# The weights' setup made part of the attention's program, with its maxima over partitions by PE and VectorE

## What is computed

```python
def attn(x, Wv, Wo, Wg, Wb):            # x is normalized
    rk = heads(x); rk = rk / max(norm(rk), 1e-12)
    wk = rk one position later, zeros first
    v = heads(x @ Wv.T); gate = sigmoid(x @ Wg.T); beta = sigmoid(x @ Wb.T)
    for t in time:                      # S is 32 x 32 for each head
        err = (v[t] - wk[t] @ S) * beta[t]
        S = S + outer(wk[t], err)
        o[t] = (rk[t] @ S) * gate[t]
    return o @ Wo.T

def ffn(x, weight, gamma_w, beta_w):
    xn = layernorm(x, eps=1e-3) * gamma_w + beta_w
    beta = mean(abs(weight)); w_q = clip(round(weight / (beta + 1e-5)), -1, 1)
    g = max(abs(xn))                    # over the whole tensor
    return clip(xn * 128 / g, -128 + 1e-5, 128 - 1e-5) @ w_q * (g * beta / 128)
```

## Time and profile before

| | us |
|---|---|
| median of 3 runs | 2226.49 |
| lowest, highest | 2221.43, 2229.44 |
| the profiled execution | 2225.45 |
| its span (first to last instruction) | 2223.7 |
| mean granted TensorE clock of it | 0.972 |

### The profile page before, as it was taken

One profiled execution on the slowest core, in us unless ns is written; L12 is line 12 of the kernel. 1 busy time (PEld: TensorE's weight loads), 2 busy tenths in 40 slices (PEclk: granted clock), 3 DMA queues, 4 the chain that ended last, 5 costly groups with the idle time before them and its releaser, 6 DMA issues. The chain is left out here.

```text
span 2223.7 us, 124254 instructions
## 1 busy us (share of the span) xinstructions
PE 2071.3 (93%) x50216; PEld 1310.2 (59%) x50216; DVE 1976.8 (89%) x5810; ACT 1759.7 (79%) x3756; POOL 1726.0 (78%) x3099
## 2 busy tenths in 40 slices
PE   1689999999999999999999999999999987599997
PEld 1356666666666666666666666666666654355554
DVE  5388999999999999999999999999999993688886
ACT  3668888888888888888888888888888744477775
POOL 2678989989999999999898999998999854244443
PEclk7789999999999999999999999999999998799999
DMA  3123333333333333333333333333333322588885
GB/s 95 45 69 79 99 100 101 100 99 101 100 100 100 100 102 103 103 101 100 99 100 100 100 102 99 101 100 101 99 102 96 88 80 73 180 228 228 228 228 126
DMA packets 171997, 247.78 MB, mean 111 GB/s; under 512 B 54904, under 2 KB 54912, under 8 KB 171424
## 3 DMA queue, kind: packets, MB, share of 16 engines
q1 hardware_dynamic: 171424, 239.85, 40.3%
HBM read 104.40 MB, written 67.11 MB: 77 GB/s over the span
## 5 line engine op out<-in xcount | busy, mean ns | idle before, releaser
L805 DVE TENSOR_TENSOR ps_elim<-ps_elim,sys 128x30 f32<-128x30 f32 (+14 forms) x1920 | 547.7, 331 | 0.7
L813 DVE TENSOR_TENSOR sys<-sys,ps_elim 128x30 f32<-128x30 f32 (+14 forms) x1920 | 539.9, 321 | 1.0
L937 PE MATMUL ps_v<-wv,xt 128*128 128x512 f16 x1536 | 431.5, 391 | 20.5 <-DMA kbd<-kt 14.4
L937 PE MATMUL ps_y<-wo,ot 128*128 128x512 f16 x1536 | 401.4, 384 | 11.0 <-DVE x L866 10.4
L974 PEld LDWEIGHTS ps_chain<-rhs,t_t 32*32 32x32 f32 x16384 | 255.1, 144 | 110.1 <-issue 103.6
L974 PE MATMUL ps_chain<-rhs,t_t 32*32 32x32 f32 x16384 | 282.9, 218 | 5.8 <-DVE rhs L834 4.8
L711 ACT ACTIVATE state<-ps_s 128x512 f32<-128x512 f32 x128 | 76.5, 598 | 239.1 <-PE ps_s L1036 237.0
L1323 PE MATMUL ps_f<-wq,f_xq 128*128 128x512 f16 x1024 | 242.6, 381 | 6.8 <-DVE f_xq L1289 6.8
L1036 PEld LDWEIGHTS ps_s<-err,key_b 32*32 32x32 f32 x16384 | 169.7, 105 | 116.4 <-issue 115.5
L937 PEld LDWEIGHTS ps_v<-wv,xt 128*128 128x128 f16 x1536 | 121.5, 99 | 155.1 <-issue 82.8
L1036 PE MATMUL ps_s<-err,key_b 32*32 32x32 f32 x16384 | 201.0, 195 | 8.8 <-issue 8.7
(11 more groups left out here) (163 smaller groups left out, 5038.6 us busy)
## 6 DMA issues: line engine op xcount, KB each, us to landing
x_in<-in_L_attn_x SPq DMA_DIRECT2D x512, 64.0 KB
kbd<-kt SPq DMA_DIRECT2D x512, 64.0 KB, 2.4
key_bd<-key_t SPq DMA_DIRECT2D x512, 64.0 KB, 2.2
x_res<-in_L_attn_x SPq DMA_DIRECT2D x512, 64.0 KB, 2.1
x_scratch<-x SPq DMA_DIRECT2D x128, 256.0 KB, 2.3
f_x<-x_scratch SPq DMA_DIRECT2D x32, 1024.0 KB, 7.8
out<-f_res SPq DMA_DIRECT2D x128, 256.0 KB, 4.0
gate<-gates SPq DMA_DIRECT2D x128, 7.9 KB
```

What stands on the lines that cost most here:

```text
L805: dve.tensor_tensor(tmp, factors(r, c, first, end)[:, c - first:C - 1 - first, c - first:c - first + 1].to_broadcast(shape), sys[:, r, c:c ...
L813: dve.tensor_tensor(dst, dst, tmp, ALU.add).then_inc(elim_done[r], 1)
L937: last = pe.matmul(out, lhs[:, a, kb, :], weights[:, w, kb, :], start=(i == 0), stop=(i == 3 * KB - 1))
```

## The change

`setup` goes as a function and as a block. Its work is done by the engines' programs of `attention`: `run` takes a second function, `setup(j)`, which each engine calls after its `step(None, j)` and which holds setup work for a few values of j; some work stands ahead of the loop.

- SP loads Wv first, then x tile 0, Wb and Wg, x tile 1, Wo, x tile 2, the FFN's weight, gamma and beta.
- PE turns Wv and the gates' weights ahead of the loop, into four banks (and one of the elimination's) that the pipeline doesn't use yet, and Wo after step -8.
- ACT scales Wv and the gates' weights straight into their high float16 parts after step -10, and Wo after step -5, with the sums of its rows as an accumulated output.
- DVE reduces Wv and the gates' weights and makes their scales and low parts ahead of the loop. It reduces Wo and the FFN's weight after step -9, makes the scale of Wo and rounds the FFN's weight after step -6 (two operations in place of three), centres and splits Wo after step -5, and centres `wq` and fills `z_ends` after step -4.
- A maximum over partitions is a transpose of the column by PE into one row, a reduction of the row by DVE, and a matmul by ones; the sum is one matmul by a matrix of ones. Both leave their result in PSUM. `partition_all_reduce` is gone.
- GpSimd writes the constants and clears `kbd` and `key_bd` ahead of the loop, makes the mask after step -10, clears `state` after step -8 and makes `attn_eps` after step -5.
- The raw weights lie in buffers that the pipeline doesn't use yet (`key_t`, `x1`, `pred`, `o_g`, part of `key_b`, `t_t`). GpSimd waits in the Gram stage of tile 4 for the low parts of Wo.
- Waits at the first use: of Wv's parts in the first `value`, of the gates' scale and parts in step -7, of Wo's parts in the first output.

The diff, cut to its core, with eight columns of indentation taken off inside functions:

```diff
-def setup(nc, io, k):
...
+raw_v = key_t[:, 0:4, :, :].rearrange("p k h c -> p k (h c)")
+raw_o = key_t[:, 4:8, :, :].rearrange("p k h c -> p k (h c)")
+raw_f = x1
+raw_g = pred
+gb_rows = o_g
+wt_o = key_b[:, 4:8, :]
+below = t_t[:, :, :, :, :].rearrange("p r i a h -> p r (i a h)").rearrange("p r (k n) -> p (r k) n", n=D)
...
+turn_banks = (ps_chain, ps_s, ps_y, ps_zn)
+ones = err[:, 0, 0:P]
+top_rows, top_all, rows_bank = ps_elim[1][0:1, 0:2 * P], ps_elim[1][:, 2 * P:2 * P + 4], ps_elim[1][:, 3 * P:3 * P + 2 * KB]
...
+def run(step, setup):
     for j in range(FIRST, LAST + 1):
         step(None, j)
+        setup(j)
...
+    def setup(j):
+        if j == FIRST:
+            sp.dma_start(raw_g[0:H, :], io["Wb"]).then_inc(loaded["g"], 16)
+            sp.dma_start(raw_g[H:2 * H, :], io["Wg"]).then_inc(loaded["g"], 16)
+        elif j == FIRST + 1:
+            sp.dma_start(raw_o, io["Wo"].rearrange("(k p) n -> p k n", p=P)).then_inc(loaded["o"], 16)
+        elif j == FIRST + 2:
+            sp.dma_start(raw_f[:, :, :], io["Wf"].rearrange("(k p) n -> p k n", p=P)).then_inc(loaded["f"], 16)
+            sp.dma_start(gb_rows[0:KB, 0:P], io["gamma"].rearrange("(k p) -> k p", p=P)).then_inc(loaded["rows"], 16)
+            sp.dma_start(gb_rows[KB:2 * KB, 0:P], io["beta"].rearrange("(k p) -> k p", p=P)).then_inc(loaded["rows"], 16)
+            for dst, src in ((k["gamma_bc"], io["gamma"]), (k["beta_bc"], io["beta"])):
+                sp.dma_start(dst[:, :], src.rearrange("(a n) -> a n", a=1).to_broadcast([P, D])).then_inc(loaded["bc"], 16)
...
-                sp.wait_ge(s["first_gate"], 1)
+                sp.wait_ge(s["consts"], 8)
...
+    sp.dma_start(raw_v, io["Wv"].rearrange("(k p) n -> p k n", p=P)).then_inc(loaded["v"], 16)
+    run(step, setup)
...
-    pool.memset(state[:, 0, :], 0.0).then_inc(s["state_done"], 1)
+    pool.memset(k["ident"][:, :], 0.0).then_inc(s["ident_s"], 1)
+    pool.memset(k["neg_mask"][:, :], -1.0).then_inc(s["mask_s"], 1)
...
+    pool.memset(gates[:, BODY - 1, :], 0.0).then_inc(s["consts"], 1)
+    pool.memset(ones, 1.0).then_inc(s["consts"], 1)
+    pool.wait_ge(s["ident_s"], 1)
+    pool.affine_select(out=k["ident"][:, :], in_=k["ident"][:, :], compare_op=ALU.not_equal, fill=1.0,
+                       base=0, pattern=[[-1, P]], channel_multiplier=1).then_inc(s["ident_s"], 1)
+    pool.memset(kbd[:, :, :, :, :], 0.0).then_inc(s["kbd_zero"], 1)
-    pool.memset(kbd[:, :, :, :, :], 0.0).then_inc(s["kbd_zero"], 1)
-    pool.memset(gates[:, BODY - 1, :], 0.0).then_inc(s["first_gate"], 1)
+    pool.wait_ge(s["consts"], 7)
...
+    def setup(j):
+        if j == -LAG_XHAT:
+            for b in range(B):
+                m = k["neg_mask"][C * b:C * b + C, :]
+                pool.wait_ge(s["mask_s"], 1 + b)
+                pool.affine_select(out=m, in_=m, compare_op=ALU.is_gt, fill=0.0, base=0,
+                                   pattern=[[1, C]], channel_multiplier=-1).then_inc(s["mask_s"], 1)
+            pool.wait_ge(s["mask_s"], 1 + B)
+        elif j == -LAG_NORM:
+            pool.memset(state[:, 0, :], 0.0).then_inc(s["state_done"], 1)
+        elif j == -LAG_GRAM + 1:
+            pool.wait_ge(s["scale_vg"], 4)
+            pool.wait_ge(s["scale_of"], 4)
+            pool.tensor_tensor(attn_down[:, :], down[:, 0:1], down[:, 2:3], ALU.mult).then_inc(s["attn_s"], 1)
+            pool.wait_ge(s["attn_s"], 1)
+            pool.tensor_tensor(attn_sq[:, :], attn_down[:, :], attn_down[:, :], ALU.mult).then_inc(s["attn_s"], 1)
+            pool.wait_ge(s["attn_s"], 2)
+            pool.tensor_scalar(k["attn_eps"][:, :], attn_sq[:, :], LN_EPS, None, ALU.mult).then_inc(s["attn_s"], 1)
+            pool.wait_ge(s["attn_s"], 3)
...
+            if n == 4:
+                pool.wait_ge(s["o_low"], KB)
...
+            if n == 0:
+                act.wait_ge(s["scale_vg"], 5)
...
+    def setup(j):
+        if j == -LAG_XHAT:
+            act.wait_ge(s["scale_vg"], 4)
+            for kb in range(KB):
+                act.wait_ge(s["v_turned"], kb + 1)
+                nc.scalar.activation(k["wv"][:, 0, kb, :], turn_banks[kb][:, :], ACT.Identity,
+                                     scale=down[:, 0:1]).then_inc(s["v_high"], 1)
+            act.wait_ge(s["g_turned"], 1)
+            nc.scalar.activation(k["wgb"][:, 0, :, :].rearrange("p k n -> p (k n)"), ps_elim[0][:, 0:KB * 2 * H], ACT.Identity,
+                                 scale=down[:, 1:2]).then_inc(s["g_high"], 1)
+        elif j == -LAG_GRAM + 1:
+            act.wait_ge(s["scale_of"], 4)
+            for kb in range(KB):
+                act.wait_ge(s["o_turned"], kb + 1)
+                nc.scalar.activation(wt_o[:, kb, :], turn_banks[kb][:, :], ACT.Identity, scale=down[:, 2:3],
+                                     accum_out=wo_sum[:, kb:kb + 1]).then_inc(s["o_scaled"], 1)
+            act.wait_ge(s["o_turned"], KB + 1)
+            nc.scalar.activation(k["gb_cols"][:, :], rows_bank, ACT.Copy).then_inc(s["o_scaled"], 1)
...
+    def scales(c, end, done, ready):
+        dve.wait_ge(*ready)
+        dve.tensor_scalar(top_floor[:, c:end], top_all[:, c:end], 1e-30, None, ALU.max).then_inc(done, 1)
+        dve.wait_ge(done, 1)
+        dve.tensor_scalar(pow2[:, c:end].bitcast(I32), top_floor[:, c:end].bitcast(I32), 0x7F800000, None,
+                          ALU.bitwise_and).then_inc(done, 1)
+        dve.wait_ge(done, 2)
+        dve.tensor_scalar(unit[:, c:end], pow2[:, c:end], 2.0, None, ALU.mult).then_inc(done, 1)
+        dve.wait_ge(done, 3)
+        dve.reciprocal(down[:, c:end], unit[:, c:end]).then_inc(done, 1)
+        dve.wait_ge(done, 4)
+    def low(parts, bank, scale, ready, done):
+        dve.wait_ge(*ready)
+        dve.scalar_tensor_tensor(out=parts[1], in0=bank, scalar=scale, in1=parts[0],
+                                 op0=ALU.mult, op1=ALU.subtract).then_inc(done, 1)
+    def setup(j):
+        if j == -LAG_TURN:
+            dve.wait_ge(loaded["o"], 16)
+            dve.tensor_reduce(top[:, 2:3], raw_o.rearrange("p k n -> p (k n)"), AX_X, ALU.max,
+                              apply_absolute_value=True).then_inc(s["top_of"], 1)
+            dve.wait_ge(loaded["f"], 16)
+            dve.tensor_reduce(top[:, 3:4], raw_f[:, :, :].rearrange("p k n -> p (k n)"), AX_X, ALU.add,
+                              apply_absolute_value=True).then_inc(s["top_of"], 1)
+        elif j == -LAG_NORM:
+            dve.wait_ge(s["all_of"], 1)
+            dve.tensor_reduce(topmost[0:1, 2:3], top_rows[:, 0:P], AX_X, ALU.max).then_inc(s["top_of"], 1)
+        elif j == -LAG_GRAM:
+            dve.wait_ge(s["all_of"], 2)
+            dve.tensor_scalar(k["w_mean"][:, :], top_all[:, 3:4], 1.0 / (D * D), None, ALU.mult).then_inc(s["thr_s"], 1)
+            dve.wait_ge(s["thr_s"], 1)
+            dve.tensor_scalar(thr[:, 0:1], k["w_mean"][:, :], Q_EPS, 0.5, ALU.add, ALU.mult).then_inc(s["thr_s"], 1)
+            dve.tensor_scalar(thr[:, 1:2], k["w_mean"][:, :], Q_EPS, -0.5, ALU.add, ALU.mult).then_inc(s["thr_s"], 1)
+            scales(2, 3, s["scale_of"], (s["all_of"], 2))
+            dve.wait_ge(s["thr_s"], 3)
+            dve.tensor_scalar(below, raw_f[:, :, :], thr[:, 1:2], None, ALU.is_lt).then_inc(s["wq_s"], 1)
+            dve.wait_ge(s["wq_s"], 1)
+            dve.scalar_tensor_tensor(out=k["wq"][:, :, :], in0=raw_f[:, :, :], scalar=thr[:, 0:1], in1=below,
+                                     op0=ALU.is_gt, op1=ALU.subtract).then_inc(s["wq_s"], 1)
+        elif j == -LAG_GRAM + 1:
+            dve.wait_ge(s["o_scaled"], KB + 1)
+            dve.tensor_scalar(wo_mean[:, :], wo_sum[:, :], -1.0 / D, None, ALU.mult).then_inc(s["o_high"], 1)
+            dve.wait_ge(s["o_high"], 1)
+            for kb in range(KB):
+                dve.tensor_scalar(k["wo"][:, 0, kb, :], wt_o[:, kb, :], wo_mean[:, kb:kb + 1], None,
+                                  ALU.add).then_inc(s["o_high"], 1)
+            for kb in range(KB):
+                dve.wait_ge(s["o_high"], kb + 2)
+                dve.scalar_tensor_tensor(out=k["wo"][:, 1, kb, :], in0=wt_o[:, kb, :], scalar=wo_mean[:, kb:kb + 1],
+                                         in1=k["wo"][:, 0, kb, :], op0=ALU.add, op1=ALU.subtract).then_inc(s["o_low"], 1)
+        elif j == -LAG_GRAM + 2:
+            dve.wait_ge(s["wq_s"], 2)
+            dve.tensor_reduce(wq_sum[:, :], k["wq"][:, :, :], AX_X, ALU.add).then_inc(s["wq_s"], 1)
+            dve.wait_ge(s["wq_s"], 3)
+            dve.tensor_scalar(wq_mean[:, :], wq_sum[:, :], -1.0 / D, None, ALU.mult).then_inc(s["wq_s"], 1)
+            dve.wait_ge(s["wq_s"], 4)
+            for kb in range(KB):
+                dve.tensor_scalar(k["wq"][:, kb, :], k["wq"][:, kb, :], wq_mean[:, kb:kb + 1], None,
+                                  ALU.add).then_inc(s["wq_s"], 1)
+            dve.memset(k["z_ends"][:, 0, :], -3.0e38).then_inc(s["max_done"], 1)
+            dve.memset(k["z_ends"][:, 1, :], 3.0e38).then_inc(s["min_done"], 1)
```

(63 more changed lines are left out.)

203 lines of the change are left out of this document (19 added, 184 removed).

## The result

The changed kernel takes 2188.07 us in the median of four runs (2184.31 to 2197.02), the kernel before beside it 2225.85 (2221.43 to 2229.44). The ratio is 0.9849 with an interval of 0.9826 to 0.9871: 33.6 us are gained, between 28.7 and 38.7. Forecast were 24.3 us and a time of 2202.2, in a range of 2196 to 2212. The direction is right, the gain is more than a third larger than said, and the time lies outside the range.

A forecast was written before the change was run, and what follows sets the result against it. PE was taken to bound the steady steps, so only the front could gain: start 30.3, minus 0.4 early filling, 4.8 late DVE blocks and 0.8 waiting for GpSimd, gives 24.3 us, so 2202.2 us, range 2196 to 2212.

The forecast's parts named there:

- What bounds the kernel, and that the front slides: PE bounds the steady steps, DVE 4% behind; only the front is edited, and everything behind it slides by its gain.
- The start, 30.3 us: Pipeline's front: ACT takes up tile 3 at 18.6 us instead of 48.94, a shift of 30.3 us (28.3 to 32.1).
- The new maxima cost nothing: Front: maxima by PE and DVE take 1.47 us; scales ready at 13.5 to 14, before ACT asks at 15.6.
- Steps -9 to -6: Early filling: the first value matmul loses 0.4 us or 0; step -6's DVE block, 5.2 us, is hidden with 3 left.
- Steps -5 and -4: Late filling: DVE blocks of 7.4 and 4.6 us before the elimination, less 7.3 of idle, leave 4.7 us lost.
- one wait: Steps -5 and -4: DVE's one-input operations stand still while GpSimd works; 0.8 us added, bounds 0 and 3.
- the four gaps: DVE's idle before the gates of steps -4 to -1: 4.19, 2.06, 0.42 and 0.63 us, 7.3 in all, absorbing moved work.
- An unchanged step: Steady steps: from the state of tile 0 on, everything comes 24 us earlier with the step's length unchanged.
- rival A: Filling: everything hides, DVE's moved blocks cost nothing; gain 29 to 33 us, 2193.5 to 2197.5; chance 0.08.
- B: Steps -5 and -4: some ten DVE operations each wait for GpSimd (1.16); 8 us more, gain 16, about 2210; chance 0.13.
- C: Front: no gain, the setup's chain stays in front; gain 0 to 7 us, about 2223; chance 0.04.
- D: Steady steps: PE's granted clock stays at its half level longer; at nine steps 12 us slower, 2238; chance 0.03.

The follow-up runs named there:

- again_before: The kernel before, unchanged, profiled a second time; ACT's copy of tile 4's state starts at 194.88 us, and 2015.9 us follow to the end.
- the three padded ones: Kernel before with idle PE transposes added in its setup: twelve (2217.03 us in one execution; again, 2222.12 us, ratio 0.9960) or six (2226.66 us, 0.9983).
- again_after: The changed kernel, unchanged, profiled and timed again: 2184.48 us, ratio 0.9863 to the kernel before.
- after_pe_pads: The changed kernel with twelve useless PE transposes ahead of its loop; one profiled execution, share of late hand-overs 0.14, no time given.
- after_held: The changed kernel with its front held late by five extra, waited-for loads of Wv: 2216.94 us against 2222.33, ratio 0.9970 to the kernel before.
- more_late: The changed kernel with two more reductions of wq on DVE behind step -4: 2192.05 us, ratio 0.9880 to the kernel before.
- earlier_blocks: The changed kernel with late setup work one step forward, wq's centring behind the last tile, z_ends filled before the loop: 2181.86 us, ratio 0.9833 to before.

## Why the prediction was right and wrong

*What bounds the kernel, and that the front slides.* Right. State 4, averaged over the executions with the attention's old start (before, again_before, the three padded ones: 196.9), and over after, again_after and after_pe_pads (170.1), shifts by 26.8 us. At state 0, ahead of the stretch in which the clock scatters, the same executions have 143.8 and 118.9: 24.9 us. It is of this mark that the prediction says "everything 24 us earlier".

*The start, 30.3 us.* It measured 30.0 at the sum of tile 3. The parts: tile 2 summed at 12.95 (forecast 12.0), ACT at Wv's scaling at 16.40 (15.6), its block 2.53 us (3.0), tile 3 at 18.93 (18.6). Errors of 0.8 and -0.5 nearly cancel.

*The new maxima cost nothing.* Right: 1.50 us against 1.47 of the earlier trace rows, scales at 13.23 (13.5 to 14), 3.2 us of cover. But the sentence on what they replace, an operation that "costs DVE an idle of 1.04 us", read the operation only where it was hidden. The change was weighed without asking what GpSimd's operation would have cost in its new place: 26 us. It made no difference to the sum, since the change takes it away; as a reading of why the change has two halves it missed the point.

*Steps -9 to -6.* The first value matmul shifted by 30.1; the 0.4 of loss did not come. The reductions ended at 25.27 (24.7), and PE was through with Wo at 28.9, for which 29.0 was forecast. There two errors cancel: its transposes began at 25.77, not 25.1, and took 3.2 us, not 3.9. Block -6 is hidden with 2.84 us of cover left, where 3 were forecast.

*Steps -5 and -4.* Forecast 7.4 and 4.6 us. Measured, from the gates' end to the last operation: 2.38 of waiting and 6.33 of work, 8.7 in all, and 5.5 (73.17 to 78.69). That is 2.2 us more than the blocks' forecast; another 0.8 had been set aside for one wait beside GpSimd. The rows are GpSimd's operation beside DVE's first of the block, then the four low parts of Wo and the four centrings of wq (min/median/max ns), each with the x_part of GpSimd that runs beside them:

```profile
59.48 1.05 POOL L381 TENSOR_TENSOR key_b<-key,gates 128x512 f32<-128x512 f32 x1
L760 DVE SCALAR_TENSOR_TENSOR wo<-key_b,w_small,wo x4: 739/743/1648, 62.2 to 65.1; 128x512 f16<-128x512 f32 x4
62.30 1.64 POOL L405 TENSOR_TENSOR x_part<-x_hat,x_part 128x512 f16<-128x512 f32 x1 [1.61 <-ACT x_hat L512]
L769 DVE TENSOR_SCALAR wq<-wq,w_small x4: 341/352/1171, 75.6 to 77.3; 128x512 f16<-128x512 f16 x4
75.50 1.16 POOL L405 TENSOR_TENSOR x_part<-x_hat,x_part 128x512 f16<-128x512 f32 x1
```

The first operation of the block took 1.07 us, not 0.17, and ended with GpSimd's (60.55 and 60.53). One low part took 1.65, the others 0.74 to 0.75; one centring took 1.17, the others 0.34 to 0.36. So three operations waited, once each, 2.6 us in all, where one wait was forecast. GpSimd's x_part was held up as well, 1.64 us for 1.16. The low parts cost more than the forecast 0.57 even when nothing held them, since they are another operation than the wide subtraction of the earlier trace rows: 0.4 us over the four. The wait for ACT was 0.8 us shorter than forecast. Against all this stood more slack than the four gaps of the earlier trace rows. At the gates of tile 4 the shift is 24.5 us in the two executions of the result, where 24.3 were forecast. That nearness is luck: over the executions named above it is 22.8 (110.6 and 87.9).

*"An unchanged step" behind it.* This is the step that failed. The sum puts everything behind the front at nothing, because the change "adds no work to the steady steps". That is true and was not enough. The steady steps got shorter by 0.05 us in the mean and 0.09 in the median, 6 us over the tiles and 6.7 by after_held (3.1 to 10.2). About 4 of them are the hand-over from PE to ACT. Why the mix of late and early starts changed stays open, and no row of the profile before could price it.

A smaller error lies ahead of it. The sum took the loss at DVE's gates for final. It was larger there than forecast, and a part of it came back: the shift grows from 22.8 at the gates of tile 4 to 24.9 at state 0. The moved and the lengthened blocks point the same way: of 7.4 us freed 5.2 are left at state 0, of 4.2 added 3.1. The delay was DVE's and not PE's: from the gates of tile 4 to state 0 PE had 488 matmuls to run in before and 436 in after (the number in the first bracket):

```profile
111.31:144.96 33.65, 25.10 (x488) 14.47 (x486) 32.22 (x112) 21.97 (x49) 23.65 (x41) 0.85 0.27 69
86.78:118.19 31.41, 21.20 (x436) 12.84 (x437) 31.03 (x111) 17.25 (x37) 23.52 (x41) 0.84 0.23 57
```

From state 0 to state 4 the shift grows by another 1.9 us. The granted clock in this stretch was 0.95 in the mean of the five old starts and 0.98 in that of the three new ones, and by the lengths given above that is worth about as much. Since it differs as much between executions of one kernel, nothing shows that the change brought it. So at state 0 the sum of the front was right to 0.6 us, from errors that cancel. 24.9, 1.9 and 6.7 make 33.5; the first comparison gave 33.6, the second 30.4, each to within about 5 us.

*The range.* Its gain ended at 29, and at 30.5 with a part of rival A taken in. The front alone (24.9 to 26.8) lies well inside it. What lies outside is the part of the steady steps, and the scatter of two medians of three or four runs: their difference is 37.8, where the ratio says 33.6.

*The rivals.* A (everything hides, 29 to 33 us) names the right size for the wrong reason: the blocks do cost, as more_late and earlier_blocks show. B (the exclusion bites, 8 us more) had the mechanism right and the count wrong: three waits of 0.8 to 0.9 us in place of ten of 1.16. The exclusion is larger in a place that nobody waits for: the cast at L777 takes 5.25 us, from 1.85 to 7.10, beside GpSimd's two memsets, and took 0.22 in the earlier trace rows. The Trainium skill, "SBUF — State Buffer", section "Who interferes with whom", lets a cast enter a two-port mode, and has DVE in such a mode and GpSimd exclude each other for a whole instruction; by that rule, the trace agrees, with 5.25 against 0.22 us. The landing of Wv hides it here: the reduction behind the cast begins at 6.53, and began at 6.71 in the earlier trace rows. C did not come. Nor did D: PE's granted clock in the stretches 40 to 80, 80 to 120 and 120 to 160 us is 0.81, 0.83 and 0.96, where before had 0.61, 0.79 and 0.87, so nothing is paid back there, and the steady stretch is at 1.00 in both. That the clock moves state 4 by up to 3 us between executions was in none of the rivals.

## What to carry to other kernels

An operation that looks cheap because it stands where its engine is idle has no price yet: put it where the engine is needed and read it again, for merging a setup into a pipeline moves every such cover away. Take a loss in a filling pipeline as final only at the engine that the steady state waits for; some of what a helper engine loses can come back before that. Read the granted clock of a filling stretch beside its length, before two executions are compared at its end. And when a program changes ahead of a long loop, expect a few tenths of a per cent of the loop to move with it in either direction; hold the new front back to the old start, or pad the old one, before the difference is put down to the edit.

## What the runs showed of the hardware

`partition_all_reduce`, 0.37 to 0.47 us in the trace, kept GpSimd idle for 13 to 17 us wherever it stood in the attention, 6 to 10 us in front and 7 behind, and state 0 was 14 us late even with a result that nobody reads. In the kernel before, where GpSimd had been idle for 12.9 us, it started 0.2 us behind its input, and only the 7 us behind it show.

Some operations of DVE stood still beside one of GpSimd: one of four took 1.17 us in place of 0.34, one of four 1.65 in place of 0.74, one took 1.07 in place of 0.17, and a cast beside two memsets 5.25 in place of 0.22.

The stretch of the filling from state 0 to state 4 took 50.7 us at a granted clock of 1.00 and up to 54.2 at 0.91, and the clock there differed between executions of one kernel.

ACT's copy that waits for PE's last matmul of a state started either 0.04 or 0.19 us behind it, in a mix that followed the number of matmuls that PE runs ahead of its loop: up to 50223 in all, 0.38 to 0.67 of the late kind, from 50225 on 0.09 to 0.25. A late start lengthens the step by 0.09 us. What makes the difference is open. Twelve idle transposes brought 5 to 13 us, as much as many edits that one would time, and only about 4 of them are accounted for by this hand-over.
